# A fused cross-attention and feed-forward block: fp16 parts turned by DMA instead of TensorE, and later slots

## What is computed

```
q = rms_norm(layernorm(x)) * q_norm_w            # 16 heads of 32
k = rms_norm(ctx) * k_norm_w ;  v = ctx          # 4 groups of 32
q, k = rotary(q), rotary(k)
p = softmax(causal(q k^T / sqrt(32)))            # 16 heads x 128 x 128
x = x + concat_heads(p v) @ w_out.T
h = relu(layernorm(x) @ w_up + b_up + lora)      # 512 -> 2048, 4-bit weights
x = x + h @ w_down + b_down + lora               # 2048 -> 512
```

## Time and profile before

| what | value |
|---|---|
| median of three runs | 566.35 us |
| the profiled execution | 565.46 us, span 563.7 us |
| PE busy | 513.3 us (91%) |
| DVE / ACT / POOL busy | 339.1 / 264.4 / 206.2 us |
| mean granted clock of TensorE | 0.973 |
| DMA packets | 31.89 MB, mean 57 GB/s |

### The profile page before, as it was taken

One profiled execution on the slowest core, in us unless ns is written; L12 is line 12 of the kernel. 1 busy time (PEld: TensorE's weight loads), 2 busy tenths in 40 slices (PEclk: granted clock), 3 DMA queues, 4 the chain that ended last, 5 costly groups with the idle time before them and its releaser, 6 DMA issues.

```text
span 563.7 us, 12632 instructions
## 1 busy us (share of the span) xinstructions
PE 513.3 (91%) x4968; PEld 366.1 (65%) x4968; DVE 339.1 (60%) x1058; ACT 264.4 (47%) x820; POOL 206.2 (37%) x238
## 2 busy tenths in 40 slices
PE   0257788799999999999999999999999999999997
PEld 0125435475777676767676868686868686868683
DVE  1876535454676767676767676767676767463441
ACT  1456838546453535454545454545454545343110
POOL 3393755802525252525252525252525252222100
PEclk9999659799999999999999999999999999999999
DMA  9960713101203030403031303031302020200000
GB/s 179 296 159 2 212 58 108 38 3 33 58 11 80 12 80 12 80 12 80 14 78 11 81 15 76 13 79 12 79 20 72 10 58 11 57 2 20 2 21 19
DMA packets 59772, 31.89 MB, mean 57 GB/s; under 512 B 48288, under 2 KB 50608, under 8 KB 59664
## 3 DMA queue, kind: packets, MB, share of 16 engines
q1 hardware_dynamic: 56864, 30.58, 22.3%
q10 hardware_dynamic: 2768, 0.34, 0.5%
q0 software_dynamic: 80, 0.16, 0.1%
HBM read 16.39 MB, written 4.19 MB: 37 GB/s over the span
## 4 chain that ended last, share of the span: by engine, by line
PE 82%; POOL 6%; issue 4%; DMA 2%; SPq 2%; DVE 2%; ACT 2%; POOLq 0%; DVEq 0%
PE ff L682 31%; PE ff L697 29%; PE tb L663 7%; PE tb L545 4%; PE tb L652 3%; PE sb L644 2%; DMA big<-in_L_ffn_w_up_q 2%; POOL big L335 2%; PE ff L545 2%; POOL big L332 1%; POOL pr L361 1%; PE kxb L545 1%; PE ff L590 1%; PE ff L605 1%; ACT pr L478 1%
## 5 line engine op out<-in xcount | busy, mean ns | idle before, releaser
L682 PE MATMUL ff<-xnT_hi,wu_hi 128*128 128x128 f16 x1024 | 174.0, 219 | 2.0 <-ACT wd_lo L453 1.1
L361 POOL TENSOR_TENSOR pr<-pr,rinv 128x512 f32<-128x512 f32 x64 | 78.8, 1232 | 264.5 <-DVE rinv L826 264.5
L682 PE MATMUL ff<-xnT_hi,wu_lo 128*128 128x128 f16 x1024 | 173.9, 219 | 0.0
L682 PE MATMUL ff<-xnT_lo,wu_hi 128*128 128x128 f16 x1024 | 173.8, 219 | 0.0
L697 PE MATMUL ff<-wd_hi,x 128*128 128x512 f16 x512 | 152.4, 379 | 0.0
L682 PEld LDWEIGHTS ff<-xnT_hi,wu_hi 128*128 128x128 f16 x1024 | 100.1, 98 | 14.4 <-DVE z L845 11.7
L513 ACT ACTIVATE x<-z 128x512 f16<-128x512 f32 x64 | 40.5, 632 | 133.4 <-DVE z L845 133.4
L682 PEld LDWEIGHTS ff<-xnT_lo,wu_hi 128*128 128x128 f16 x1024 | 100.2, 98 | 0.3
L682 PEld LDWEIGHTS ff<-xnT_hi,wu_lo 128*128 128x128 f16 x1024 | 100.2, 98 | 0.0
L478 ACT ACTIVATE pr<-pr,nmax 128x128 f32<-128x128 f32 x256 | 99.2, 393 | 0.0
L697 PE MATMUL ff<-wd_lo,x 128*128 128x512 f16 x256 | 97.0, 379 | 0.0
(11 more groups left out here) (136 smaller groups left out, 679.2 us busy)
## 6 DMA issues: line engine op xcount, KB each, us to landing
xt<-in_x SPq DMA_DIRECT2D x16, 256.0 KB, 3.0
big<-in_L_ffn_w_up_q SPq DMA_DIRECT2D x4, 1024.0 KB, 13.7
big<-in_L_ffn_w_down_q SPq DMA_DIRECT2D x4, 1024.0 KB, 5.7
out<-y SPq DMA_DIRECT2D x16, 256.0 KB, 2.0
kvt<-in_ctx SPq DMA_DIRECT2D x16, 64.0 KB, 2.5
wd_lo<-in_L_xattn_w_out SPq DMA_DIRECT2D x1, 1024.0 KB, 13.7
wd_hi<-in_L_ffn_w_up_lora_b SPq DMA_DIRECT2D x3, 128.0 KB, 8.2
wd_hi<-in_L_xattn_q_norm_w SPq DMA_DIRECT2D x1, 256.0 KB, 6.3
```

Source lines behind the costliest of these rows:

```text
L361: pool.tensor_tensor(pr[:, m], pr[:, m], rinv[:, p, 4 * m:4 * m + 4].unsqueeze(2).broadcast_to([P, NG, P]), ALU.mult).then_inc(probs, 1)
L682: last = pe.matmul(bank[:, P * h:P * h + P], a[:, m, cols], b[:, p, m, :], start=(h == 0 and m == 0 and i == 0), stop=(m == KC - 1 and i = ...
```

## The change

Probabilities and the second norm are no longer turned by TensorE in fp32. ACT writes the high fp16 part, POOL (probabilities) or DVE (norm) the low one, and SP issues a DMA transpose of both parts together: four per batch for the probabilities (`pT`, 1024 columns each) and one for the norm (`xnT`, 1024 columns). The values get a scale from their sum of squares (a small fp32 product with ones, a power on POOL) and are split as well, so that `R_PV` is three fp16 products per group in place of one fp32 product. ACT instead of DVE centres both norms, with the sign turned; the scale of the first norm goes into the splits of q and k. The copies `prT`, `xnT_hi` from PSUM and the bank `kxb` go. `big` gives 8 KB per partition to the parts of the probabilities, so the ring of the weight groups has three buffers and group 3 is no longer issued before the slots. From batch 1 on, the projection and what follows it are one slot later, the up and down layers also, and the norm's turn (`R_TURN2`) is gone: `R_NORM2` stands three slots ahead of `R_UP`.

```diff
-R_PT = ((8, 15), (9, 16), (10, 17), (11, 18))
-R_PV, R_OSPLIT, R_PROJ, R_X1, R_POW2, R_NORM2, R_TURN2 = (12, 20), (13, 21), (13, 21), (14, 22), (14, 23), (15, 24), (16, 25)
-R_UP, R_DOWN = (18, 26), (22, 30)
-R_RESULT = (26, 34)
+R_PSPLIT = ((8, 15), (9, 16), (10, 17), (11, 18))
+R_VSUM, R_VSPLIT = (5, 12), (6, 14)
+R_PV, R_OSPLIT, R_PROJ, R_X1, R_POW2, R_NORM2 = (13, 20), (14, 21), (14, 22), (15, 23), (15, 23), (16, 24)
+R_UP, R_DOWN = (18, 27), (22, 31)
+R_RESULT = (26, 35)
-RING = 4
+RING, W_RING = 4, 3
...
             def load_group(g):
-                if g >= 4:
-                    sp.wait_ge(w_turned, 4 * (g - 3))
+                if g >= W_RING:
+                    sp.wait_ge(w_turned, 4 * (g - W_RING + 1))
...
+                n = at(s, R_NORM2)
+                if n is not None:
+                    sp.wait_ge(xn_high, n + 1)
+                    sp.wait_ge(xn_low, n + 1)
+                    if n > 0:
+                        sp.wait_ge(up_done, 4 * n)
+                    sp.dma_start_transpose(xnT[:], xn_parts[:].rearrange("p a c -> p (a c)")).then_inc(xn2_turned, 16)
...
+                for m in range(NN):
+                    n = at(s, R_PSPLIT[m])
+                    if n is not None:
+                        sp.wait_ge(p_high, 4 * n + m + 1)
+                        sp.wait_ge(p_low, 4 * n + m + 1)
+                        if n > 0:
+                            sp.wait_ge(heads_out, n)
+                        sp.dma_start_transpose(pT[:, m], p3[:, m].rearrange("p g a t -> p (g a t)")).then_inc(p_turned, 16)
-                for g in range(4, 8):
-                    if TILE_AT[4 * (g - 4) + 3] == s:
+                for g in range(W_RING, 8):
+                    if TILE_AT[4 * (g - W_RING) + 3] == s:
                         load_group(g)
...
+            def probabilities_low(s):            # POOL, last in its slot
+                        pool.wait_ge(p_high, 4 * n + m + 1)
+                        pool.tensor_tensor(p3[:, m, :, 1, :], pr[:, m], p3[:, m, :, 0, :], ALU.subtract).then_inc(p_low, 1)
+            def values_low(s):
+                    pool.tensor_tensor(v3[:, 1, :], vs[:], v3[:, 0, :], ALU.subtract).then_inc(v_low, 1)
+            def value_scales(s):
+                    pool.tensor_tensor(v_scales[:, n % 2, :], v_arg[:].broadcast_to([P, 2]), v_powers[:],
+                                       ALU.pow).then_inc(v_scaled, 1)
...
+            def centre(s):                       # ACT; DVE's centre is gone
+                    act.activation(xc[:], xt[:, n % RING, :], ACT.Identity, scale=-1.0,
+                                   bias=mv[:, n % 2, 0:1]).then_inc(x_centred, 1)
+                        act.wait_ge(exps, 4 * n + m + 1)      # after the exponentials of a group
+                        act.activation(scaled_sum[:, 4 * m:4 * m + 4], rsum[:, p, 4 * m:4 * m + 4], ACT.Copy,
+                                       scale=1.0 / P_TOP).then_inc(sums_scaled, 1)
+                        act.activation(p3[:, m, :, 0, :], pr[:, m], ACT.Copy).then_inc(p_high, 1)
+                    act.activation(vs[:], kvt[:, n % RING, :], ACT.Identity,
+                                   scale=v_scales[:, n % 2, 0:1]).then_inc(v_sized, 1)
+                    act.activation(v3[:, 0, :], vs[:], ACT.Copy).then_inc(v_high, 1)
+                    act.activation(xn2[:], x1[:, p, :], ACT.Identity, scale=-1.0, bias=mv2[:, p, 0:1]).then_inc(xn2_ready, 1)
+                    act.activation(xn_parts[:, 0, :], xn2[:], ACT.Identity, scale=inv2[:, p:p + 1]).then_inc(xn_high, 1)
-                        act.activation(prT[:, :, m, :], tb[m % 2][:].rearrange("p (g t) -> p g t", g=NG),
-                                       ACT.Copy).then_inc(probsT, 1)
...
+                    pe.matmul(vb[:, 0:1], ones[:], ssq[:, n % 2:n % 2 + 1], start=True, stop=True).then_inc(v_summed, 1)
-                        for g in range(NG):
-                            last = turn(tb[m % 2][:, P * g:P * g + P], pr[:, m, g, :], start=True, stop=True)
-                    for m in range(KC):
-                        last = turn(kxb[:, P * m:P * m + P], xn2[:, P * m:P * m + P], start=True, stop=True)
-                    pe.wait_ge(probsT, 4 * n + 4)
-                    for g in range(NG):
-                        d = slice(HD * g, HD * g + HD)
-                        last = pe.matmul(tb[1][d, :], kvt[:, n % RING, d], prT[:, g].rearrange("p n t -> p (n t)"),
-                                         start=True, stop=True)
+                    pe.wait_ge(p_turned, 16 * (4 * n + 4))
+                    pe.wait_ge(v_high, n + 1)
+                    pe.wait_ge(v_low, n + 1)
+                    for i, (a, b) in enumerate(((0, 0), (1, 0), (0, 1))):
+                        for g in range(NG):
+                            d = slice(HD * g, HD * g + HD)
+                            last = pe.matmul(tb[1][d, :], v3[:, a, d], pT[:, :, 2 * g + b, :],
+                                             start=(i == 0), stop=(i == 2))
...
+            def second_norm_low(s):              # DVE
+                    dve.scalar_tensor_tensor(xn_parts[:, 1, :], xn2[:], inv2[:, n % 2:n % 2 + 1], xn_parts[:, 0, :],
+                                             ALU.mult, ALU.subtract).then_inc(xn_low, 1)
-                    dve.tensor_scalar(xn2[:], x1[:, p, :], mv2[:, p, 0:1], inv2[:, p:p + 1],
-                                      ALU.subtract, ALU.mult).then_inc(xn2_ready, 1)
```

More of the change, by code:

```diff
@@ L21 @@
 W_TOP, A_TOP, X2_TOP = 2.0 ** 13, 2.0 ** 10, 2.0 ** 14
+P_TOP, V_TOP = 2.0 ** 14, 2.0 ** 15
 BIG = 1e30
@@ L159, in build @@
         b_in = sem("b_in")
-        wq_in = [sem(f"wq_in{i}") for i in range(4)]
+        wq_in = [sem(f"wq_in{i}") for i in range(W_RING)]
         down_bias_in, b_flat_in = sem("down_bias_in"), sem("b_flat_in")
@@ L318, in _ @@
             pool.memset(minus_half[:], -0.5).then_inc(pool_consts, 1)
-            pool.memset(ones8[:], 1.0).then_inc(pool_consts, 1)
+            pool.memset(ones[:], 1.0).then_inc(ones_set, 1)
+            pool.memset(v_powers[:, 0:1], -0.5).then_inc(v_powers_set, 1)
+            pool.memset(v_powers[:, 1:2], 0.5).then_inc(v_powers_set, 1)
             def rotary_tables(*tables):
@@ L363, in probabilities @@
                                            ALU.mult).then_inc(probs, 1)
+            def probabilities_low(s):
+                for m in range(NN):
+                    n = at(s, R_PSPLIT[m])
+                    if n is not None:
+                        pool.wait_ge(p_high, 4 * n + m + 1)
+                        pool.tensor_tensor(p3[:, m, :, 1, :], pr[:, m], p3[:, m, :, 0, :], ALU.subtract).then_inc(p_low, 1)
+            def values_low(s):
+                n = at(s, R_VSPLIT)
+                if n is not None:
+                    pool.wait_ge(v_high, n + 1)
+                    pool.tensor_tensor(v3[:, 1, :], vs[:], v3[:, 0, :], ALU.subtract).then_inc(v_low, 1)
+            def value_scales(s):
+                n = at(s, R_VSUM)
+                if n is not None:
+                    pool.wait_ge(v_arg_ready, n + 1)
+                    if n >= 2:
+                        pool.wait_ge(o_low, n - 1)
+                    pool.tensor_tensor(v_scales[:, n % 2, :], v_arg[:].broadcast_to([P, 2]), v_powers[:],
+                                       ALU.pow).then_inc(v_scaled, 1)
             def cosines(s):
@@ new lines, in second_norm_high @@
+            def second_norm_high(s):
+                n = at(s, R_NORM2)
+                if n is not None:
+                    p = n % 2
+                    act.wait_ge(x1_moments, n + 1)
+                    if n > 0:
+                        act.wait_ge(xn_low, n)
+                    act.activation(xn2[:], x1[:, p, :], ACT.Identity, scale=-1.0, bias=mv2[:, p, 0:1]).then_inc(xn2_ready, 1)
+                    act.wait_ge(xn2_ready, n + 1)
+                    act.wait_ge(norm2, n + 1)
+                    if n > 0:
+                        act.wait_ge(xn2_turned, 16 * n)
+                    act.activation(xn_parts[:, 0, :], xn2[:], ACT.Identity, scale=inv2[:, p:p + 1]).then_inc(xn_high, 1)
@@ L533, in _ @@
                     act.activation(ident16[:], ident, ACT.Copy).then_inc(ident_cast, 1)
-                    act.activation(barrier[:], mask, ACT.Copy, scale=-1.0).then_inc(barrier_set, 1)
                     act.activation(minus16[:], ident, ACT.Copy, scale=-1.0).then_inc(minus_cast, 1)
@@ L549, in spread_tops @@
                 turn(sbk[1][0:8, 0:P], tops[:], start=True, stop=True).then_inc(tops_turned, 1)
-                pe.wait_ge(pool_consts, 2)
+                pe.wait_ge(ones_set, 1)
                 pe.wait_ge(diag8_ready, 1)
-                pe.matmul(tb[0][:, 0:8], ones8[:], diag8[:], start=True, stop=True).then_inc(tops_spread, 1)
+                pe.matmul(tb[0][:, 0:8], ones[0:8, :], diag8[:], start=True, stop=True).then_inc(tops_spread, 1)
             def wout_turn(m):
@@ L993, in _ @@
                 queries(s)
+                values(s)
```

187 lines of the change are left out of this document (100 added, 87 removed).

## The result

The changed kernel takes **588.07 us** (median of 4 runs, 587.63 to 589.75), against 566.18 beside it: ratio 1.0379, 95% interval 1.0337 to 1.0421. It is slower; 549 was forecast, and 588 lies outside the range of 536 to 566.

What follows compares the result with a forecast made beforehand. PE was taken to bound the steady periods, with a small wait from POOL's loop after the change. Span 563.7 + 11 prologue - 2 first period - 25 steady - 1.2 drain = 546.5, execution 548.3, median 549 us; range 536 to 566.

Steps and rivals of the forecast that it cites:

- PE's sum: Steady period: PE's work falls from 28.1 to 25.75 us, through turns gone, cheaper values' products and a new product with ones.
- POOL's chain: Steady period: POOL's operations after a projection, from the power to the last low part, end 13.9 us after it.
- the last lands 3.0 us later, at 16.9: Steady period: last transpose of probabilities lands 0.6 us after PE needs it, making the period 26.3 us (26.2 used).
- rival C: Steady period: PE's wait for turned probabilities halves its clock; period 30.8, 609 us; chance 0.13 together with values' products running serially.
- rival B: Steady period: POOL's loop binds harder, through slower fp16 operations or late landings; period 27.4, 565 us; chance 0.12.
- don't fill the queue: Steady period: all transposes are 7680 columns and take 9 us of 26 on the DMA queue.
- The rate of 219 GB/s: DMA engines' rate inside the queries' transpose in the earlier trace; a group of 1024 columns, 256 KB, takes 1.2 us.
- Carried slot by slot, the first up layer starts near 121.5, +11 us: Prologue: late weight loads and added work delay the first up layer from 110.34 us; bounds +3 and +17.
- The stalls: Prologue: DVE held 9 us before tile 12, costing PE 5.5 us, and 9.4 us without PE work around tile 24.
- 2.7 us for turns no longer on the path: Prologue credit: eight groups turned at about 1 us each at half clock, a third of it on the path.
- 2 us of a POOL wait: Prologue credit: 2 us that PE no longer waits on POOL's product.
- The first period: Between first and second up layer, 38.0 us before: saves 2 us, from five pieces of turns partly not on the path.

Runs made afterwards that it cites:

- e4: Changed kernel with weight groups 3 to 7 loaded from ACT's queue and the products with the values one slot later: 553.7 us, ratio 0.974.
- e2: Changed kernel with the late weight loads (groups 3 to 7) issued on ACT's queue instead of SP's: 574.18 us, ratio 1.0115.
- e1: Kernel before with only the weight ring cut from four to three buffers, group 3 loaded in SP's slot 4: 587.72 us, ratio 1.0341.
- e6: Changed kernel with the loads of x and ctx issued five slots later, away from the transposes of probabilities: 585.36 us, ratio 1.0301.
- e10: Kernel before with two more DMA transposes per batch on SP's queue that nothing waits for: 566.38 us, ratio 1.0002.
- e5: Changed kernel with the store of y issued two slots later, so it no longer follows the last transpose: 588.23 us, ratio 1.0356.
- e8: e4 with the store of y two slots later and the loads of x and ctx five slots later: 553.75 us, ratio 0.9782.

## Why the prediction was wrong

**PE's sum: nearly right.** The turns are gone. The twelve products with the values took 0.83 us (forecast 0.7; the four row groups do run side by side) and the two with `ones` 0.17 (0.15). PE's work in the undisturbed periods of e4 is 25.92 to 26.19 us against a forecast of 25.75, so the gain was put 0.2 to 0.4 us too high; with 0.2 us of wait for the output's low part the period is 26.35. The change's gain in PE is real: e4 collects it.

**POOL's chain: right in its end.** Last low part at 342.8, 13.9 us after the projection, as forecast. That is in part luck: inside it single steps were off both ways (base of the output 1.67 for 1.45, products 1.04 for 1.31, low parts 1.12 to 1.61 for 1.31).

**The failed step of the steady state: "the last lands 3.0 us later, at 16.9".** It landed 3.1 to 5.0 us after issue, 18.7 us after the projection in the loop shown; PE came to it at 16.4, as counted. The interpolated 3.0 is right for a transpose that nothing disturbs (3.07 to 3.26, five of thirteen), and wrong for the eight that an instruction packet met. That and the issue at 14.2 for 13.9 made PE's idle time 1.62 us a period instead of 0.45. In three periods the clock fell as rival C describes, at 1.6 us each where it gave 3.1, 0.37 a period. With 0.25 of PE's work, this gives 28.0 us a period instead of 26.2, 23.2 us in thirteen. It is rival B's mechanism, late landings, with C's on top in three places; B's 27.4 was too low. I had written that the transposes "don't fill the queue". They don't, and they were late all the same.

The rate of 219 GB/s in the earlier trace rows is not the most that a transpose reaches: in the changed kernel, with only a transpose of probabilities under way, a stretch reads

```profile
341.00:341.50 0.50, 0.50 (x13) 0.50 (x11) 0.00 (x0) 0.08 (x1) 0.50 (x1) 1.00 1.27 289
```

The Trainium skill (Advanced Engine Details and Errata, X-Bar Transpose) expects 350 to 400; neither row comes near it. What the forecast lacked was not the rate but the stalls between issue and landing.

**The failed step of the prologue: "Carried slot by slot, the first up layer starts near 121.5, +11 us".** The stalls themselves were right: DVE idle 9.9 us before tile 12 (forecast 9), the projection held for 8.95 us (forecast 9.4), tile 16 6.1 us late (forecast 5.5). I had counted 14.9 us for them, and taking the loads off SP (e2) gives 15.0 back; that the two agree so closely is in part luck, since I overlooked that group 5 stands behind three transposes of probabilities, issued at 82.38 instead of 68.14 (DVE waited 12.75 us for it). The failed term is what I took off again, 2.7 us for turns no longer on the path and 2 us of a POOL wait: the measured 20.35 us has no room for it. Whether the turns gave anything at all no run separates; the rest of the change costs 5.4 us that e2 and e4 still show and that I had put at nothing. The projection at the lower clock is among them (4.86 us in the chain against 3.0 for the same one in the kernel before); what lowers the clock there stays open.

**The first period** grew by 4.0 us where I took 2 off: about 2 us are the first up group at the lower clock (4.64 for 2.84 us), as in e1; the other 2, which only the rest of the change brings, are open.

**The account:** from 549 to 588 are 39 us: 9.3 in the prologue, 6.0 in the first period, 23.2 in the steady state, 0.7 in the drain. Two edits of placement, in e4, take back 34 of them.

## What to carry over

When a turn on an engine is replaced by a DMA transpose, plan with its landing at its worst, not its least or its median, and place the consumer one slot beyond that: here one slot was worth 19.5 us. When a landing is late, look at which other queues had a packet under way. Before a ring loses a buffer, look at what its loads stand behind on their queue; a load behind an instruction that waits for compute is only as early as that wait, and a free queue was worth 14 us. A gain in the bound engine's sum shows only where nothing new must arrive in time for it.

## What the hardware showed that I had not expected

Transposes land 1 to 2 us late now and then, while a few packets that are under way take over a microsecond each and hardly any other begins (3 to 10 GB/s). Each late one among the last transposes of the changed kernel and of e6 (13 of 24), and each of the eleven in e10's comparison, had a packet of an instruction queue beside it; the eleven last transposes without one landed within 0.2 us of each other. More transposes make it more frequent (2 against 9 in 300 us in e10, with 38 instruction packets in both); moving plain transfers does not help (e5, e8). What would, fewer or otherwise timed instruction packets, no run tries.

A wait of PE under 2 us was sometimes enough for the lower clock, and a longer one sometimes not: after 1.83 us (at 263.27) the clock fell, after the 2.4 us before 347.69 it did not.
